# The first block of a two-layer fp32 product chain: A12 from a second queue, both operands rounded on DVE, passes in another order

## What is computed

```
x = x + x @ W0.T + (x @ A0[i0]) @ B0.T * 0.5
x = x + x @ W1.T + b + (x @ A1[i1]) @ B1[i1] * 2
```

## Time and profile before

| | us |
|---|---|
| median of 3 runs | 294.34 |
| lowest, highest run | 293.6, 295.23 |
| the profiled execution, whole time | 294.61 |
| the profiled execution, span of the profile | 293.0 |
| PE busy | 287.8 (98%) |
| DVE busy | 186.9 (64%) |
| ACT busy | 131.8 (45%) |

### The profile page before, as it was taken

How to read it: one execution, slowest core, us unless ns; L and a number is a source line. 1 busy time by engine, 2 the same in 40 slices (tenths; PEclk the granted TensorE clock), 3 DMA queues, 4 the chain that set the end, 5 groups by cost and what they waited for, 6 DMA issues and landing times.

```text
span 293.0 us, 3807 instructions
## 1 busy us (share of the span) xinstructions
PE 287.8 (98%) x1323; PEld 236.6 (81%) x1323; DVE 186.9 (64%) x280; ACT 131.8 (45%) x213; POOL 73.8 (25%) x96
## 2 busy tenths in 40 slices
PE   7999999999999999999999999999999999999995
PEld 3888878888778888888888888888888888888884
DVE  3599699999879969997483373364265266256020
ACT  4673238695981474724345244234334333424100
POOL 2603331531024220071151061071070060151000
PEclk9999999999999999999999999999999999999999
DMA  6999532226232442325518017026125224312003
GB/s 204 353 373 340 76 54 38 73 36 107 39 124 73 77 88 65 115 91 166 155 39 270 26 64 249 21 89 225 46 91 195 75 92 159 110 61 82 3 0 143
DMA packets 16342, 34.33 MB, mean 117 GB/s; under 512 B 2498, under 2 KB 4674, under 8 KB 15300
## 3 DMA queue, kind: packets, MB, share of 16 engines
q1 hardware_dynamic: 12708, 28.46, 29.2%
q0 software_dynamic: 3616, 5.64, 10.0%
HBM read 20.06 MB, written 8.39 MB: 97 GB/s over the span
## 4 chain that ended last, share of the span: by engine, by line
PE 97%; DMA 1%; ACT 0%; SPq 0%; DVE 0%; issue 0%
PE bank L983 52%; PE bank L879 7%; PE bank L852 7%; PE bank L856 6%; PE bank L861 6%; PE bank L972 5%; PE bank L990 2%; PE bank L989 2%; PE bank L925 2%; PE bank L894 2%; DMA rA<-w 1%; PE bank L952 1%; PE bank L909 1%; PE bank L910 1%; PE bank L933 1%; PE bank L932 1%
## 5 line engine op out<-in xcount | busy, mean ns | idle before, releaser
L454 ACT ACTIVATE zo<-bank 128x512 f32<-128x512 f32 x32 | 19.1, 597 | 83.0 <-PE bank L983 59.7
L817 DVE TENSOR_TENSOR zo<-bank,zo 128x512 f32<-128x512 f32 x32 | 22.0, 690 | 47.6 <-PE bank L990 26.8
L983 PE MATMUL bank<-MM,X 128*128 128x512 f32 x192 | 46.5, 390 | 0.0
L983 PEld LDWEIGHTS bank<-MM,X 128*128 128x128 f32 x192 | 35.9, 188 | 7.4
L359 POOL TENSOR_TENSOR xraw<-xraw 128x512 f32<-128x512 f32 x7 | 9.0, 1289 | 72.9 <-DVE X L629 72.9
L629 DVE TENSOR_TENSOR SH<-xraw,SH 128x512 fp32r<-128x512 f32 x32 | 24.8, 811 | 2.8 <-ACT SH L454 2.8
L454 ACT ACTIVATE SH<-xraw 128x512 fp32r<-128x512 f32 x32 | 19.2, 625 | 14.1 <-PE bank L990 7.2
L629 DVE TENSOR_TENSOR X<-xraw,X 128x1024 fp32r<-128x1024 f32 x16 | 19.4, 1220 | 9.5 <-ACT X L454 9.5
L983 PE MATMUL bank<-sa,SH 128*128 128x512 f32 x96 | 23.2, 391 | 0.0
L983 PE MATMUL bank<-sc,SH 128*128 128x512 f32 x96 | 23.2, 391 | 0.0
L983 PE MATMUL bank<-sf,SH 128*128 128x512 f32 x96 | 23.1, 389 | 0.0
(11 more groups left out here) (183 smaller groups left out, 557.0 us busy)
## 6 DMA issues: line engine op xcount, KB each, us to landing
xraw<-xT SPq DMA_DIRECT2D x8, 1024.0 KB, 5.5
out<-zo SPq DMA_DIRECT2D x32, 256.0 KB, 2.0
rB<-w1T SPq DMA_DIRECT2D x16, 256.0 KB, 9.0
rA<-w SPq DMA_DIRECT2D x15, 256.0 KB, 8.8
rA<-rA POOLq DMA_DIRECT2D x8, 256.0 KB, 4.1
Rraw<-Rg SPq DMA_DIRECT2D x16, 128.0 KB, 3.7
rawA<-la SPq DMA_DIRECT2D x8, 128.0 KB, 2.2
Rraw<-lbs POOLq DMA_DIRECT2D x16, 64.0 KB, 3.3
```

What stands on the lines that cost most here:

```text
L454: return eng.activation(o, i, ACT.Copy, scale=scale)
L817: ins = eng.tensor_tensor(zo[z][:, :], bank[bk][:, :], zo[z][:, :], ALU.add)
L983: ins = mm(bk[:, :], x(px, k), m(pm, k), start=(start and n == 0 and k == 0), stop=(stop and n == 2 and k == H - 1), skip_group_check=True)
```

## The change

Four things are edited, all at the start of the program.

1. The loads of A12's block 0 (both pieces) are issued by ACT, ahead of its table load, and no longer by SP. SP issues B21's block 0 and goes on at once with block 1. The function `load` is moved out of SP's program, so that both can call it.
2. The H part of B21's block 0 is made by DVE (new step `HB`, a plain copy) and its L part by DVE behind it (`LB`). ACT makes of block 0 only piece 1 of A12.
3. The twelve matmuls of m2's block 0 run pass by pass (`first_rows`): four H x H, four H x L, four L x H, in place of three passes for each bank.
4. NWARM is 6 in place of 7.

The diff:

```diff
--- before.py
+++ after.py
@@ -14,7 +14,7 @@
 K = D // 128
 H = K // 2
 U = RA + RB
-NWARM = 7
+NWARM = 6
 
 
 class Order:
@@ -48,8 +48,9 @@
 def loads():
 
     out = []
-    for k in range(H):
-        out += [("B21", k, 0)] + [("A12", k, p) for p in range(2 if k == 0 else 1)]
+    out += [("A12", 0, 0), ("B21", 0, 0), ("A12", 0, 1)]
+    for k in range(1, H):
+        out += [("B21", k, 0), ("A12", k, 0)]
     for k in range(H):
         out += [("B11", k, 0), ("A11", k, 0)]
     out.append(("B0", 0, 0))
@@ -84,8 +85,8 @@
 
     act_prog, dve_prog = [("TAB",)], [("WM",)]
 
-    act_prog += h([("B21", 0, 1)]) + [("HP", 1)]
-    dve_prog += [("HP", 0)] + l_([("B21", 0, 1)]) + [("LP", 0), ("LP", 1)]
+    act_prog += [("HP", 1)]
+    dve_prog += [("HP", 0), ("HB",), ("LB",), ("LP", 0), ("LP", 1)]
     for k in range(1, H):
         act_prog += h([("B21", k, k + 1), ("A12", k, k + 1)])
         if k == H - 1:
@@ -170,7 +171,7 @@
 
     H_at = {(n[1], k): v for n, v in act_at.items() if n[0] == "H" for k in range(n[2], n[3])}
     L_at = {(n[1], k): v for n, v in dve_at.items() if n[0] == "L" for k in range(n[2], n[3])}
-    H_at["A12", 0], L_at["A12", 0] = act_at["HP", 1], dve_at["LP", 1]
+    L_at["A12", 0], L_at["B21", 0] = dve_at["LP", 1], dve_at["LB",]
 
     XBANK, ZBANK, YBANK, DBANK, UBANK = (5, 1), 6, 7, 0, 4
 
@@ -277,6 +278,16 @@
 
         def x_quarters():
             return (xraw[:, k:k + H, c:c + 128] for c in (0, 128) for k in (0, H))
+
+        def load(eng, q, k, p):
+            if q == "B0":
+                o, i = rawB0[:, :, :], lb
+            else:
+                r, c = H * (q in ("A12", "A22", "B21", "B22")), 512 * (q in ("A21", "A22", "B12", "B22"))
+                lo, hi = PIECES[p] if (q, k) == ("A12", 0) else (0, 512)
+                o = raw[q][:, k, lo:hi]
+                i = (w0 if q[0] == "A" else w1T)[128 * (r + k):128 * (r + k + 1), c + lo:c + hi]
+            eng.dma_start(o, i).then_inc(d_w[q, k, p], 16)
 
         block = ctx.enter_context(nc.Block())
 
@@ -377,18 +388,9 @@
 
         @block.sync
         def _(eng):
-            def load(q, k, p):
-                if q == "B0":
-                    o, i = rawB0[:, :, :], lb
-                else:
-                    r, c = H * (q in ("A12", "A22", "B21", "B22")), 512 * (q in ("A21", "A22", "B12", "B22"))
-                    lo, hi = PIECES[p] if (q, k) == ("A12", 0) else (0, 512)
-                    o = raw[q][:, k, lo:hi]
-                    i = (w0 if q[0] == "A" else w1T)[128 * (r + k):128 * (r + k + 1), c + lo:c + hi]
-                eng.dma_start(o, i).then_inc(d_w[q, k, p], 16)
-
             for l in loads():
-                load(*l)
+                if l[:2] != ("A12", 0):
+                    load(eng, *l)
             ia0 = nc.values_load_multi_w_load_instructions(
                 i0[0:1, 0:B], engines=(mybir.EngineType.SP,), min_val=0, max_val=NL - 1)[1]
 
@@ -485,6 +487,8 @@
                 elif q == "M21":
                     eng.wait_ge(s_dve, max(L_at["S4", k] for k in range(lo, hi)))
 
+            for p in range(2):
+                load(eng, "A12", 0, p)
             for op in act_prog:
                 k = op[0]
                 if k == "TAB":
@@ -634,6 +638,12 @@
                     lo, hi = PIECES[op[1]]
                     eng.wait_ge(d_w["A12", 0, op[1]], 16)
                     ins = eng.tensor_copy(slots["b"][:, 0, 0, lo:hi], raw["A12"][:, 0, lo:hi])
+                elif k == "HB":
+                    eng.wait_ge(d_w["B21", 0, 0], 16)
+                    ins = eng.tensor_copy(slots["d"][:, 0, 0, :], raw["B21"][:, 0, :])
+                elif k == "LB":
+                    eng.wait_ge(s_dve, dve_at["HB",])
+                    ins = rest(slots["d"][:, 1, 0, :], raw["B21"][:, 0, :], slots["d"][:, 0, 0, :])
                 elif k == "LP":
                     lo, hi = PIECES[op[1]]
                     if op[1] == 0:
@@ -837,31 +847,41 @@
 
                 sa, sb = home(a), home(b)
                 for k in range(H):
-                    pieces = (a, k) == ("A12", 0)
+                    if (a, k) == ("A12", 0):
+                        first_rows(sa, sb, banks)
+                        continue
                     eng.wait_ge(s_act, H_at[b, k])
-                    if not pieces:
-                        eng.wait_ge(s_act, H_at[a, k])
+                    eng.wait_ge(s_act, H_at[a, k])
                     for i in range(H):
                         bk = bank[banks + i]
                         if k == 0 and first is not None:
                             eng.wait_ge(*first[i])
-                        if pieces and i == 0:
-                            eng.wait_ge(s_dve, dve_at["HP", 0])
-                        elif pieces and i == 2:
-                            eng.wait_ge(s_act, act_at["HP", 1])
                         mm(bk[:, :], sa[:, 0, k, cols(i)], sb[:, 0, k, :], start=(start and k == 0), stop=False,
                            skip_group_check=True)
                         if i == 0:
                             eng.wait_ge(s_dve, L_at[b, k])
                         mm(bk[:, :], sa[:, 0, k, cols(i)], sb[:, 1, k, :], start=False, stop=False, skip_group_check=True)
-                        if pieces and i % 2 == 0:
-                            eng.wait_ge(s_dve, dve_at["LP", i // 2])
-                        elif i == 0:
+                        if i == 0:
                             eng.wait_ge(s_dve, L_at[a, k])
                         ins = mm(bk[:, :], sa[:, 1, k, cols(i)], sb[:, 0, k, :], start=False, stop=(k == H - 1),
                                  skip_group_check=True)
                         if k == H - 1:
                             done(ins, name, i)
+
+            def first_rows(sa, sb, banks):
+
+                for n, (x, y) in enumerate(PASSES):
+                    for i in range(H):
+                        if n == 0 and i == 0:
+                            eng.wait_ge(s_dve, dve_at["HB",])
+                        elif n == 0 and i == 2:
+                            eng.wait_ge(s_act, act_at["HP", 1])
+                        elif n == 1 and i == 0:
+                            eng.wait_ge(s_dve, dve_at["LB",])
+                        elif n == 2 and i % 2 == 0:
+                            eng.wait_ge(s_dve, dve_at["LP", i // 2])
+                        mm(bank[banks + i][:, :], sa[:, x, 0, cols(i)], sb[:, y, 0, :], start=(n == 0), stop=False,
+                           skip_group_check=True)
 
             def by_columns(name, first, a, b, banks, start):
 
```

## The result

| | before | after |
|---|---|---|
| median (us), 7 runs each | 294.38 | 295.83 |
| lowest, highest run | 293.6, 295.23 | 295.32, 296.67 |
| the profiled execution, whole time | 294.61 | 296.67 |
| its span | 293.0 | 295.1 |

The ratio after to before is 1.0055, with an interval of 1.0040 to 1.0071: slower by about 1.45 us, and clear of the noise. The forecast was 293.8 with a range up to 294.9.

A forecast was written before the change was run, and what follows sets the result against it. PE, busy 98% of the span, bounds the kernel: its side gains 0.4 to 0.7 us, the fence at m6's last row block passes 0.57; taking 0.5, 294.34 - 0.5 = 293.8 us, range 292.9 to 294.9.

The forecast's parts named there:

- The second queue: Block 0's loads: A12's piece issued 0.45 us earlier, there at about 3.8 (3.63 to 4.29); B21's at 3.95 (3.63 to 4.09).
- Rival (b): First loads: the second queue brings nothing, piece at 4.29, PE starts at 5.3, 294.3 us; chance 0.15.
- The casts on DVE: Block 0: DVE's B21 cast takes 0.5 us behind the piece's; PE starts at about 4.7 us, 0.48 earlier.
- the fence: m6's last row block: PE waits for DVE's L part; slack 0.17 us plus 0.4 from transfers passes 0.57 (0.17 to 0.87).
- The table load: ACT at the start: load now follows two issues, ends near 3.1 us in place of 2.2, and costs nothing.
- Pass by pass: m2's block 0: the two late matmul starts (0.56 and 0.54 us in place of 0.427) go, winning 0.24 us.
- One matmul on zeros less: PE's start: zeros end at 4.16 us, idle 0.54 in place of 0.59; off the path, could only change the clock.
- (a): PE's start: the clock rises much sooner; 293.4 us, or 292 to 292.5 without the fence; chance 0.15, of which 0.05 without it.
- (c): PE's start: the clock rises later, at 12.7 us, giving 295.4 us; decided by a rise after 10.3 us; chance 0.10.
- signs of being wrong: Profile after: fence moved by over 1 us, PE waiting in m2's blocks 1 to 3, or clock's rise moved over 2 us.
- The end of the transfers: Weight loads: SP's later loads issued up to 0.9 us earlier, so transfers end 0.4 us sooner (0 to 0.7).
- above 0.83: DMA engines: their average share in 2 to 6 us was to exceed 0.83, as a sign of the forecast.

The follow-up runs named there:

- e2: The kernel before with only the second queue added (ACT issues A12's two pieces, SP goes on with block 1): 296.03 us, ratio 1.0074.
- e3: The changed kernel with eleven matmuls on zeros in place of six: 294.62 us, ratio 1.0009.
- e8: The kernel before with only the new pass order in m2's first block: 294.66 us, ratio 1.0006.
- e6: The changed kernel with all loads from SP in the old order and seven matmuls on zeros: 294.96 us, ratio 1.0003.
- e5: The kernel before with six matmuls on zeros in place of seven: 294.88 us, ratio 1.0002.
- e1: The changed kernel with only the second queue taken back (SP issues all loads in the old order): 295.06 us, ratio 1.0031.
- e4: The changed kernel with SP holding block 1 back until A12's first piece is there: 295.9 us, ratio 1.0064.
- e10: The kernel of e6 with A12's first piece ahead of B21's block 0 in SP's one queue: 294.78 us, ratio 1.0019.
- e12: The kernel of e10 with nine matmuls on zeros in place of seven: 293.98 us, ratio 0.9978.

## Why the prediction was wrong

**The second queue.** This is the step that failed, and it failed in the bound. "At the latest, 4.74 - 0.45 = 4.29" took the old arrival less the issue time saved as the worst case. It reckoned the sharing between the piece and B21's block, as one stream at one rate, and nothing else. But the same edit takes two issues out of SP's queue, so block 1 of both quarters is issued 0.9 us earlier too and moves beside block 0: the prediction used that for the end of the transfers and forgot it for their beginning. Measured: piece at 5.78, not 3.63 to 4.29, and B21's block at 6.00 in e2, not 3.63 to 4.09. PE's start, 6.46, lies outside the 4.1 to 5.3. Half of the piece's 16 signals did come by 3.71; a load is there with its last signal, and that was at 5.76.

Rival (b), with the Trainium skill's rule that issuing engines are not separate DMA queues ("DMA: Bandwidth & Descriptors"), pointed the right way, since it had no gain but the issue time. It was priced by the same bound, so it ended at 294.3 and couldn't be slower. The rival that was missing is: the urgent loads are delayed by the later ones. A price of about the right size can be had from the rows, in hindsight. If all that is issued by then shared alike, block 0 is there when the 1049 KB of blocks 0 and 1 are; at the mean of 252 GB/s from 2 to 6 us that is 2 + 4.15 = 6.15 us, PE starts 0.68 behind it (the measured 5.78 to 6.46) at 6.8, and 294.34 + 1.65 = 296.0. Measured were 5.8 to 6.9 for the piece and 295.83. The signals show that the parts don't share alike, and the same sum would put the piece as late on one queue, where it mostly came at 4.1 to 4.8; so it is no bound (e3's piece came at 6.88), and that it fits is partly luck.

**The casts on DVE.** Right in the main: 0.42 us for 512 columns against the 0.5 taken, and later work wasn't pushed. PE followed the cast's end by 0.05 us (6.41 to 6.46), not by the 0.15 taken; it is the same 0.05 at the fence in e8 (47.90 to 47.95), so the slack there was nearer 0.27 us than 0.17. e6 shows nothing lost by the casts, within its 0.7%.

**The table load.** Right: it ended at 3.12 (3.1 was said) and cost nothing.

**Pass by pass.** One of the two late starts went. after's first two matmuls start at 6.46 and 7.05, still 0.59 us apart though the second has nothing to wait for; only behind them is the spacing 0.43. So 0.08 us were won in place of 0.24, and neither can be seen in e8, whose interval is 0.7% wide.

**One matmul on zeros less.** No cost by itself (e5). But the break it was to be hidden in grew from 0.59 to 2.30 us with the late operands, and e3 shows that filling such a break is worth 1.2 us there. The cover was named, and its price when gone was not.

**Rivals (a) and (c), the clock.** The time of (c), 295.4, is the nearest to what was measured, and for the wrong reason. Its deciding point was a rise later than 10.3 us. The rise was at about 12.5 in the first profile and at 10.6 in the second, so the point was passed in both, and in the first the rise moved by over 2 us, one of the prediction's signs of being wrong. But PE had started 1.3 and 1.5 us later, and the low clock cost 2.96 and 1.98 us against before's 2.18: no steady loss. As "TensorE: Matmul & The Clock Gate" of the Trainium skill says of the number of slow matmuls, it changes from run to run of one kernel; these two profiles agree, with fourteen and nine real ones. The early rise of (a) did not come in after. It came in e1 and e8, where the trace records the high clock at 4.24 and 5.29 us; the second term of the ledger was 1.13 and 0.82, and the rest was 0.4 and 1.3 us longer. The lower end given for (a), 292, is a slip: 294.34 - 2.6 is 291.7.

**The end of the transfers.** Taken at 0.4 us sooner; DVE's wait for the identity ended at 31.16 in place of 31.77, 0.61 sooner. The size was right within its range of 0 to 0.7. The share in 2 to 6 us was 0.835 on average (0.60, 1.07, 0.74, 0.93), where "above 0.83" was to show it, the same as before's 0.825: this sign was of no use.

**The fence.** Not reached in after, since PE came there no earlier than DVE. It is real (e8), though no hard cap: e1's profile has a span 1.1 us below before's, where at most 0.87 was to pass. One thing about it was left out: when PE is late, DVE is late with it. In after, DVE's L part for m6's k = 2 waits 2.60 us for ACT, which stands behind a copy of one of PE's results:

```profile
44.03 0.69 DVE L633 TENSOR_TENSOR se<-lowe,se 128x512 fp32r<-128x512 f32 x1 [2.60 <-ACT se L456]
```

The same L part began at 41.96 in before. So the 0.61 us that DVE won at 31 us were lost again by 44.

What stays open: whether six matmuls on zeros or the casts on DVE beside one queue cost the 0.3% of e1; why e4's median lies 0.8 us above its profiled execution; what the quicker runs of e3 look like inside; how much of the delay comes from the second queue as such and how much from block 1's earlier issue, since no run has the second queue with block 1 issued at its old time; and why the last signals of a load can come 2 to 3 us behind the first half.

## What to carry to other kernels

A second issuing queue doesn't put a load ahead of the others; it puts it beside them. Before moving an urgent load to it, list everything that both queues will have under way until it lands, and ask which of its bytes must move first: here the two operands needed 393 KB, and 878 KB were moved before they were there (694 in the old program). A load is there when its slowest part is, so a sum of bytes over a mean rate gives no upper bound. Where an edit takes issues out of a queue, everything behind them moves up, and that can hurt the very transfer that was to gain; holding the rest back by a wait isn't free either, as the same bytes are missed later.

## What the runs showed of the hardware

- The same 262 KB load, issued at the same 0.94 us as the first of its queue, is there at 3.63 us when the other queue is silent (before), and at 6.00 when 262 KB are issued on the other queue from 0.93 on (e2).
- The 16 signals of a 131 KB load spread over 3.40 to 4.71 us in before and over 3.60 to 5.76 in after, with eight of them by 3.60 and 3.71.
- A 131 KB load that is second in its queue arrives anywhere from 4.05 to 6.32 us in seven executions; in the two profiles where it is first (e10, and e12 at 3.32) it came at 3.36 and 3.32.
- The high clock was lost again: after eleven matmuls on zeros until 6.04 us, a break of 1.5 us and real ones from 7.56 on, the granted clock fell from 1.00 to 0.50 at 9.08 us, and PE ran 0.43 apart until 12.5 (e3).
- In after and before the granted clock reads 1.00 while the spacing of 0.43 us shows the low level: the trace's first record of the clock comes at 12.55 and 9.51 us. Of the starts of the programs, only e3's has a record of the low level.
- A DVE copy from f32 to fp32r took 0.42 us for 512 columns and 0.29 for 256; ACT takes 0.63 and 0.42 for the same.
